# Selective scan of a hybrid block: projections in two steps, B and C rows through DRAM, six decay buffers

## The reference, cut to what matters

```python
x_dbl = einsum('bkdl,kcd->bkcl', xs, x_proj_weight)          # 38 rows: 6 for dt, 16 B, 16 C
dts, Bs, Cs = x_dbl[:, :, :6], x_dbl[:, :, 6:22], x_dbl[:, :, 22:]
dt = softplus(einsum('bkrl,kdr->bkdl', dts, dt_projs_weight) + bias)
h  = h * exp(dt * A) + (dt * u) * B                          # per pixel; 192 channels x 16 states
y  = sum over states of h * C;  then + Ds * u, and the four directions are added
```

## Time and profile before

| | |
|---|---|
| profiled execution, own time | 3110.97 us |
| its span, first to last instruction | 3108.9 us |
| median of the three runs | 3111.86 us |
| scan loop: first product to last scan | 75.5 to 1541.6 us |
| VectorE busy, whole span | 2223.0 us (72%) |
| DMA read and written in HBM | 239.66 and 25.88 MB |

### The profile page before, as it was taken

One profiled execution on the slowest core, in us unless ns is written; L12 is line 12 of the kernel. 1 busy time (PEld: TensorE's weight loads), 2 busy tenths in 40 slices (PEclk: granted clock), 3 DMA queues, 4 the chain that ended last, 5 costly groups with the idle time before them and its releaser, 6 DMA issues. The chain is left out here.

```text
span 3108.9 us, 33979 instructions
## 1 busy us (share of the span) xinstructions
PE 2521.1 (81%) x9156; PEld 920.0 (30%) x9156; DVE 2223.0 (72%) x3030; ACT 1424.7 (46%) x1949; POOL 1311.6 (42%) x677
## 2 busy tenths in 40 slices
PE   4677677776677766776668689999999889999999
PEld 2111111111111111111124123232232246666766
DVE  4999999999999998999755688787878631111112
ACT  3444544445444444444456147676767522222221
POOL 1788878787788877788751100000000200000000
PEclk9777767777677777777758689999999889999999
DMA  3555555555555555555512603131313400000000
GB/s 88 144 167 165 160 152 166 154 155 159 157 168 162 166 146 152 160 152 163 152 47 80 104 2 43 23 42 24 42 23 42 87 1 6 5 5 5 5 5 10
DMA packets 101755, 286.76 MB, mean 92 GB/s; under 512 B 14878, under 2 KB 19137, under 8 KB 101569
## 3 DMA queue, kind: packets, MB, share of 16 engines
q1 hardware_dynamic: 100506, 284.94, 35.1%
q10 hardware_dynamic: 1102, 0.19, 0.0%
HBM read 239.66 MB, written 25.88 MB: 85 GB/s over the span
## 5 line engine op out<-in xcount | busy, mean ns | idle before, releaser
L528 POOL TENSOR_TENSOR hs<-hs,bc 128x1024 f32<-128x1024 f32 x384 | 900.4, 2355 | 224.9 <-DVE hs L614 224.2
L501 ACT ACTIVATE decay<-decay,a_neg 128x1024 f32<-128x1024 f32 x384 | 440.4, 1148 | 666.2 <-DMA decay<-dt_rows 652.3
L425 PE MATMUL psU<-stack,spread_sel 96*128 96x512 bf16 x768 | 361.1, 487 | 425.0 <-DVE hs L614 346.3
L1446 DVE TENSOR_REDUCE mx<-ps 128x1 f32<-128x512 f32 x864 | 539.3, 682 | 117.7 <-PE ps L1285 112.4
L558 DVE TENSOR_TENSOR psU<-psU,bc 128x512 f32<-128x512 f32 x768 | 514.4, 673 | 25.9 <-issue 13.4
L1421 ACT ACTIVATE P<-ps 128x512 f32<-128x512 f32 x768 | 417.6, 599 | 249.3 <-PE ps L1297 225.2
L614 DVE TENSOR_TENSOR_SCAN hs<-decay,psU 128x512 f32<-128x512 f32 x384 | 464.7, 1210 | 72.6 <-PE psY L387 52.4
L614 DVE TENSOR_TENSOR_SCAN hs<-decay,hs,psU 128x512 f32<-128x512 f32 x384 | 487.5, 1269 | 1.1
L387 PE MATMUL psY<-hs,state_sel 128*32 128x512 f32 x1572 | 401.5, 855 | 23.2 <-DVE Y L571 11.2
L1719 DVE SCALAR_TENSOR_TENSOR acc<-psE,gate,acc 128x192 f32<-128x192 f32 x128 | 53.4, 417 | 448.5 <-PE psE L1619 445.5
L1285 PE MATMUL ps<-ks,qs 96*128 96x512 bf16 x864 | 345.0, 404 | 34.8 <-DMA ks<-qk_parts 24.2
(11 more groups left out here) (237 smaller groups left out, 2280.3 us busy)
## 6 DMA issues: line engine op xcount, KB each, us to landing
decay<-dt_rows SPq DMA_DIRECT2D x388, 512.0 KB
stack<-parts SPq DMA_DIRECT2D x297, 64.0 KB, 5.5
dt_rows<-dt SPq DMA_DIRECT2D x33, 384.0 KB, 7.1
qs<-qk_parts SPq DMA_DIRECT2D x90, 128.0 KB, 6.7
ks<-qk_parts SPq DMA_DIRECT2D x90, 128.0 KB, 7.2
qk_parts<-qparts SPq DMA_DIRECT2D x16, 576.0 KB, 3.7
w<-in_L_ffn_w_dram SPq DMA_DIRECT2D x8, 576.0 KB, 9.9
X<-in_x_dram SPq DMA_DIRECT2D x4, 768.0 KB, 9.7
```

The lines of the kernel that those rows point to most:

```text
L425: pe.matmul(psU[:, q % UR, :], s.spread_sel[:, gg, :], stack[:, ui % 2, j, CH * pos:CH * pos + CH], start=True, stop=True).then_inc(dtu_sp ...
L501: nc.scalar.activation(decay[:, t % DR, :], decay[:, t % DR, :], ACT.Exp, scale=s.a_neg[:, col:col + 1]).then_inc(decay_ready, 1)
L528: pool.tensor_tensor(h, h, bc[:, 2 * p + r, 1, :], ALU.mult).then_inc(hc_ready, 1)
L1446: v.reduce_max(mx[:, slot, u:u + 1], ps1[:, (slot * MAXES + u) % R, :], AX.X).then_inc(max_done, 1)
```

## The change

- **Projections in two steps.** `inputs` projects x once per image and p to 128 rows `xd`: the 6 dt rows of both r at rows 0 and 32, the B and C rows at 64 and 96. `steps` projects 96 dt rows from 6 of them. The turned copy `xt` is gone: TensorE and POOL read X with a stride of 32 elements where p = 1. The folded weight is gone from `prepare`.
- **B and C by DMA.** SP stores the rows of `xd` to `bc_dram` and loads each 16 rows 8 times over into `bc`: eight loads of 512 KB per image (two in each of units 5, 6, 7 and 0).
- **GpSimd makes 2 of 12 increments.** For tiles 5 and 11 SP stores 8 rows of dt*u to `dtu_dram` and loads them repeated into `rep` (512 KB); POOL multiplies by B. VectorE has no product for these tiles, TensorE no spread; ACT writes their decay to the PSUM slots that are free.
- **Remainders from TensorE.** dt*u minus the known parts is a sum of matmuls in PSUM (`remainder`); ACT copies the middle and the low part from there. POOL's two subtractions go.
- **Parts through DRAM.** The parts are stored (384 and 192 KB) and loaded to `stack` with three DMAs of 192 KB, after a wait for the stores.
- **Ring sizes.** DR 4 to 6, HR 6 to 8. All four directions of a half are summed in psY, the term Ds*u by a matmul (`skip`), and ACT takes psY every fourth unit; the column directions' sums read `hs` with a stride of 32 elements.

```diff
-        HR, DR, UR = 6, 4, 4
+        HR, DR, UR = 8, 6, 4
+        POOL_TILES = (5, 11)
...
+                def inputs(out, nb, p, c):
+                    for h in range(2):
+                        m = pe.matmul(out, s.w_xd[:, p, h, :], turned(s.X[:, nb, h, :], p)[:, 16 * c:16 * c + 16, :],
+                                      start=(h == 0), stop=(h == 1))
+                def steps(nu, c):
+                    pe.matmul(psP[0:HC, c, :], s.w_dt[BLK * r:BLK * r + R, p, HC * f:HC * f + HC],
+                              xd[BLK * r:BLK * r + R, p, CH * c:CH * c + CH], start=True, stop=True).then_inc(z_proj, 1)
+                def remainder(c, known, ready):
+                    m = pe.matmul(psP[0:HC, c, :], s.ident[0:HC, 0:HC], dtu[:, cs], start=True, stop=False)
+                    for i in range(known):
+                        m = pe.matmul(psP[0:HC, c, :], s.minus_bf[:], parts[:, i, cs], start=False, stop=(i == known - 1))
...
+                        h = h.rearrange("p (w h) -> p h w", h=HH) if p else h.rearrange("p (h w) -> p h w", h=HH)
...
                             pool.tensor_tensor(h, h, bc[:, slot, 1, :], ALU.mult).then_inc(hc_ready, 1)
-                            if t == 2:
-                                pool.tensor_tensor(rest[:], dtu[:], parts[:, 0, :], ALU.subtract).then_inc(rest_ready, 1)
-                            if t == 5:
-                                pool.tensor_tensor(parts[:, 2, :], rest[:], parts[:, 1, :],
+                            if t + 3 in POOL_TILES:
+                                pool.tensor_tensor(rep[:], rep[:], bc[:, slot, 0, :], ALU.mult).then_inc(rep_ready, 1)
...
+                def load_rep(slot, i):
+                    src = s.dtu_dram[slot, i].unsqueeze(1).broadcast_to([DD, N, L])
+                    sp.dma_start(rep[:], src).then_inc(rep_landed, 16)
+                def load_bc(slot, which=(0, 1)):
+                        src = s.bc_dram[p, at:at + N, :].unsqueeze(0).broadcast_to([DD, N, L])
+                        sp.dma_start(bc[:, slot, i, :], src).then_inc(bc_landed[slot], 16)
...
+                sp.wait_ge(xd_stored, 32)
+                load_bc(0)
+                keep_dt(0)
+                keep_dtu(0)
                 for t in range(DR):
+                    load_dt(0, t)
+                load_rep(0, 0)
+                keep_parts(0, 0, 2, hm_stored)
+                keep_parts(0, 2, 1, lo_stored)
+                stack_up(0)
+                load_bc(1)
+                load_bc(2)
...
                         for t in range(TILES):
                             if t == TILES - DR:
                                 sp.wait_ge(dt_stored, n * 16 + 32)
                             sp.wait_ge(scan_done, n * (2 * TILES) + (2 * t + 2 + S0))
+                            if t + DR < TILES:
+                                load_dt(ui % 4, t + DR)
+                            else:
+                                load_dt((ui + 1) % 4, t + DR - TILES)
+                            if t == POOL_TILES[0]:
+                                load_rep(ui % 2, 1)
+                            if t == 1:
+                                sp.wait_ge(dtu_ready, n + 2)
+                                keep_dtu((ui + 1) % 2)
+                            if t == 2 and ui in (5, 6, 7, 0):
+                                load_bc((ui - 5) % UNITS, (0,))
+                            if t == 4 and ui in (5, 6, 7, 0):
+                                load_bc((ui - 5) % UNITS, (1,))
+                            if t == 5:
+                                keep_parts((ui + 1) % 2, 0, 2, hm_stored)
+                            if t == 6:
+                                keep_parts((ui + 1) % 2, 2, 1, lo_stored)
+                            if t == 7:
+                                sp.wait_ge(lo_stored, n * 16 + 32)
+                                stack_up((ui + 1) % 2)
+                            if t == POOL_TILES[1]:
+                                sp.wait_ge(dtu_stored, n * 32 + 64)
+                                load_rep((ui + 1) % 2, 0)
```

More of the change, by code:

```diff
@@ L346, in _ @@
                 pe.sem_inc(scan_done, S0)
[L347 removed]
+                pe.sem_inc(summed, SUM0 - 2)
                 for first in (y_taken, hc_ready):
                     pe.sem_inc(first, START)
[L351 to L366, removed]
@@ new lines, in take @@
+                def take(b, f, last):
+                    act.wait_ge(summed, last + SUM0)
+                    nc.scalar.copy(s.Y[:, b, f, :], psY[0:HC, :, :].rearrange("p c l -> p (c l)")).then_inc(y_taken, 1)
+                nc.scalar.preload_act_table_set("natural_log_exp_and_others")
+                for p in range(2):
+                    for c in range(2):
+                        act.wait_ge(xd_proj, 2 * p + c + 1)
+                        nc.scalar.copy(xd[:, p, CH * c:CH * c + CH], (psU if p else psP)[:, c, :]).then_inc(xd_ready, 1)
@@ new lines, in _ @@
+                for c in range(2):
+                    z_half(0, 0, c)
+                z_end(0)
+                act.wait_ge(dtu_ready, 1)
+                nc.scalar.copy(parts[:, 0, :], dtu[:]).then_inc(hi_ready, 1)
+                for c in range(2):
+                    part(1, 0, c, rest_ready, mid_ready)
+                for c in range(2):
+                    part(2, 0, c, tail_ready, lo_ready)
+                act.wait_ge(dt_stored, 16)
+                for c in range(2):
+                    z_half(1, 1, c)
@@ new lines, in _ @@
+                            if t == 4:
+                                act.wait_ge(hm_stored, n * 16 + 16)
+                                act.wait_ge(lo_stored, n * 16 + 16)
+                                act.wait_ge(dtu_ready, n + 2)
+                                nc.scalar.copy(parts[:, 0, :], dtu[:]).then_inc(hi_ready, 1)
+                            if t == 4 and ui % 4 == 0:
+                                take(b if ui else (b + (NB - 1)) % NB, 1 - f, n * SUB)
+                            if t == 6:
+                                for c in range(2):
+                                    part(1, n + 1, c, rest_ready, mid_ready)
@@ L619, in _, with keep_dt @@
             @block.sync
             def _(sp):
[L621 to L629 removed]
+                def keep_dt(slot):
+                    sp.dma_start(s.dt_dram[slot], dt[:]).then_inc(dt_stored, 16)
```

459 lines of the change are left out of this document (241 added, 218 removed).

## The result

The kernel after takes **3196.5 us** (median of four runs, 3167.7 to 3212.1) against 3113.3 before (3110.1 to 3120.7): ratio 1.0253, interval 1.0173 to 1.0333. It is slower, which is the direction forecast, by 1.7 to 3.3%, so clear of no change but not of 2%; it is slower by 83 us where 447 were forecast, and outside the range of 3330 to 3820. Its profiled execution is the longest of the four, 3212.1 us, and is compared with that of before, 3111.0. The four runs lie 1.4% apart, where those of before lie 0.3%.

The account below looks back on a forecast made before the run. Eight full DMA engines were taken as the bound: fifteen loads instead of twelve take a unit from 45.8 to 59.3 us, +432; start +32 and end -17 make +447 on 3109, so 3560 us, range 3330 to 3820.

Parts of the forecast that it names:

- The bound: Scan loop before: eight full DMA engines set the unit, 46.1 us summed against 45.8 measured, with VectorE close behind at 42.4.
- The price: Decay and new loads: 0.223 us a packet, 3.56 us a load on each engine; fifteen loads cost 53.4 us a unit.
- Rival A: DMA loads: speed follows demand; at 0.162 us a packet with new loads over all engines, VectorE bounds; 2955 us, chance 0.13.
- The range's low end: Whole kernel: a mean packet of 0.196 us, 52.2 us a unit, gives 3330 us.
- SP's waits: SP at tile 7, waiting for the parts to land: priced at nothing, at most some 3 us a unit (+90).
- The prediction's signs: Scan loop: VectorE busy about two thirds, its idle time ended by decay; ScalarE waiting for decay loads at most tiles.
- The buffers at nothing: Six decay and eight hs buffers: a longer queue doesn't make a full engine faster, so worth nothing.
- VectorE's freed time at nothing: VectorE in the scan: falls to 39.3 us a unit, but gains nothing because the DMA stays its cover.
- Start: Before the first spread: more loads ahead of stack, +18 us, and four bc loads behind it, +14.
- End: After the last loads: up to seven useless loads end last and the DMA stream sets the end, -17 us.
- Rival B: TensorE's sums reading hs with a stride: at four times the cost, +170 us, 3730 us; chance 0.09.
- B's first price: TensorE's strided sums at 1.9 times, from ACT's turned copy: +11 us, TensorE at 44 us a unit, hidden.

Follow-up runs that it names:

- e4: Kernel after with dt and dtu rows stored twice, so decay and rep loads use sixteen engines (bc stays on eight): 3093 us, ratio 0.9948.
- e16: Kernel after, whole, with only the tile's partitions ordered states first, so decay, rep and bc loads use sixteen engines: 3005 us, ratio 0.9652.
- e2: Kernel before with each dt row stored twice, so its decay loads go over sixteen engines: 3077 us, ratio 0.988.
- e1: Kernel before with three more 512 KB loads a unit that nobody reads: 3182 us, ratio 1.020.
- e13: Kernel before with six decay buffers instead of four (rest shares the memory of soft, adding a ScalarE wait): 3114 us, ratio 1.0018.
- e7: Kernel after without GpSimd's two increments: VectorE makes all twelve products, rep loads and dtu rows gone: 3207 us, ratio 1.0345.
- e6: Kernel after with four decay buffers instead of six: 3291 us, ratio 1.0566.
- e3: Kernel after with stack filled straight from SBUF by nine DMAs, no DRAM copy of the parts and no SP wait: 3158 us, ratio 1.0148.
- e12: Kernel after with states first (sixteen engines), stack straight from SBUF and bc loads spread over six units: 2976 us, ratio 0.9555.
- e8: Kernel after with stack straight from SBUF, dt rows stored twice for sixteen-engine decay loads, and no GpSimd increments: 3090 us, ratio 0.9957.
- e14: e12 without GpSimd's two increments, rep loads and dtu stores: 3044 us, ratio 0.9774.
- e11: Kernel before with the tile's partitions ordered states first, so decay loads use sixteen engines, dt stored once: 3073 us, ratio 0.9871.

## Why the prediction was wrong

The step that failed is the price of a packet: 0.223 us was taken as fixed, so fifteen loads were summed to 59.3 us a unit; the runs show 0.187 us and 47.8. With it failed the wait for the parts, priced at nothing.

The direction came true in part by luck: what made the kernel slower is a wait that the prediction priced at nothing, and the cost that it forecast, decay loads that hold VectorE, did not come. That the eight engines are the root held (e4, e16), by another way.

*The bound.* The reading "the eight engines are the bound" failed. Each load goes over eight engines; that held, for the new loads too (8.0 small packets). But the check that seemed to prove the bound, 46.1 us summed against 45.8 measured, could not fail: the price was the busy share times the time over the packets, so price times packets gives the time back whatever the bound is. e2 shows what the engines cost before, 0.7 us a unit, and e1 what 25% more load adds, 2.0 where the prediction's price gives 10.7. VectorE with its waits set the rest, 45.1.

*The price*, 0.223 us, fixed, was the term mis-sized. It follows the demand:

| | 8-engine loads a unit | price | unit |
|---|---|---|---|
| before, e13 | 12 | 0.223, 0.223 | 45.8, 46.0 |
| e7 | 13 | 0.213 | 47.7 |
| e6 | 15 | 0.200 | 50.8 |
| after, e1 | 15 | 0.187, 0.192 | 47.8, 47.7 |

The sum of 266 packets a unit at 0.187 gives 49.7 us, against 47.8 measured, where it had given 59.3. This too is busy time divided out and multiplied back, so it says how far the price was off, not what set the time. Rival A named this ("the loads' speed is what the demand makes of it") and its break-even, 0.172 us; I argued it down with one slow stretch in which ScalarE waited. The range's low end had stood on 0.196, a mean for which no row was given, so the measured mean fell outside. What picks one of the two prices in a stretch stays open; the number of buffers does not (e6, e13).

*SP's waits* were priced at nothing, at most 3 us a unit; SP waits 9.2 for the parts to land. The stores land after 11.7 us, where the prediction had one load in service, 3.6. Leaving the stores and this wait out (e3) gave back only 33 to 39 us, not clear of noise: straight from SBUF, too, TensorE waits 254 us for `stack`. So the late `stack` has more causes than SP's wait; the transfers ahead of it in the queue are left, and where these go over sixteen engines, in part (e4) and all (e16), the waits are 197 and 67 us. The new wait of this kernel is at `stack`. The prediction's signs had it at decay, but VectorE's idle time ends on TensorE, and ScalarE waits for 133 of 354 decay loads, not at most tiles. `stack` is issued for the next unit a few tiles before it is needed, behind loads that have six buffers of lead.

*The buffers at nothing* held for the kernel before (e13) and not for the change (94 us in e6). For tiles 5 and 11 ScalarE writes to PSUM slots and stands until VectorE has freed them, 328 us in all, 56 times. My reading is that the decay loads need the lead to ride over that and over SP's 9 us; no run separates it. With sixteen engines ScalarE stands as long (362 us in e12), and the lead is worth 14.

*VectorE's freed time at nothing* agrees with the kernel after as far as e7 and e8 can tell, which take away two loads together with it; with all loads over sixteen engines the two come to 68 us (e14).

*Start*: forecast +32, measured 34 at the third store; the first spread came at 99.3 us, not 93, so 24 of the 34 lie before it, where 18 were forecast, and 10 behind it, where 14 were. *End*: forecast -17, measured +4 at the last scan: the DMA stream did not set it.

*Rival B* is out: the sums rose from 855 to 1048 ns a matmul as a mean over both kinds, 499.6 - 401.5 = 98 us over 32 units, where B needs four times. The clock moves too (granted 0.73 before and 0.77 after in the loop), so how much of the 98 us is the stride stays open. B's first price, 1.9, compared a turned copy in fp32 with a cast to bf16; GpSimd's strided product costs 1.2 times the plain one (below). *Rival A* gave 2955 us with the new loads over all engines. They did not spread by themselves; once all loads, those of decay too, are made to, e16 and e12 take 3005 and 2976. Its VectorE term, 39.3 + 1 a unit, measured 41.7 in e12, of which 39.9 busy.

The Trainium skill ("DMA: Bandwidth & Descriptors", section "Why a DMA increments its semaphore by 16 and not by 1") gives the engine count as the largest number up to 16 that divides the slowest dimension of both sides. By that rule states first gives 16, and the trace agrees: in e12's loop 12736 small packets, less 16 for each of the 309 DMAs of `stack`, dt and `xd` and 8 for each of the 62 of `dtu_rows`, leave 7296 for 456 loads, 16.0 each.

## What to carry to other kernels

A price got by dividing busy time by work reproduces the measured time for every bound; before a sum is built on it, look whether the rate has been higher elsewhere in the trace, or add load and see whether the time follows. When a change puts more into a queue, look for the transfer with the least lead, and for the stretch where the new transfers come together: here the mean over 30 units hid that two units in eight carried the loss. And look at the order of the dimensions of a repeated load: here the order of states and channels within a tile was free, and turning it was worth 192 us on the kernel after, where the rest of the change on such loads is worth 68 (e11 to e16).

## What the runs showed of the hardware

A 4 KB packet of a repeated row load on eight engines has two prices, near 0.16 (0.162, 0.165) and near 0.25 us (0.239, 0.254), and the mix moves with the demand: 159 GB/s with 12 loads, 187 with 15 (e1), 201 after. With all sixteen engines the price is 0.278 us (66,592 packets in 1270 us at 91.2%, e12) and the rate 216 GB/s; e16, which moves the parts twice, has 226 GB/s in the same stretch. So twice the engines carried 7 to 12% more than the kernel after has, and that is still enough to end most of the waits. Whether sixteen could carry more was not measured. GpSimd's product dt*u takes 2.34 to 2.46 us where it reads X plainly and 2.84 to 2.89 us where it reads X with a stride of 32 elements (29 products between 130 and 1530 us of the kernel after).
